# Regrouping the sorted rows of a mixture of experts, its lookahead and its indirect DMAs

## The chip, the cores and the metric

The kernel runs on one core of one Trainium2 chip, in float32. The metric is the device time of one execution in microseconds. Engines: PE (TensorE, matmuls and transposes), DVE (VectorE), ACT (ScalarE), POOL (GpSimd), and SP, which issues DMAs. PEld is PE's loading of weights beside its matmuls. DMAs issued by SP and ACT have descriptors made by hardware; the indirect ones (a row for each of 128 indices) are issued by POOL, in software.

## The reference, cut to what matters

Four layers work on X, 8 sequences of 256 tokens with 128 features, 16 heads of 8. Each normalises X first and adds its result to it.

```python
x = x + attn_a(layernorm(x))     # layer 0: attention with rotated q, k, v
x = x + ffn(layernorm(x))        # layer 1
x = x + attn_b(layernorm(x))     # layer 2: attention on covariances
x = x + ffn(layernorm(x))        # layer 3, the same weights as layer 1

def ffn(x):
    h = x + attention(layer_norm(x))          # a plain attention of its own
    return h + moe(layer_norm(h))
def moe(t):                                   # t: 2048 tokens
    probs = softmax(t @ w_gate)               # 8 experts
    tw, ti = top_k(probs, 2); tw /= tw.sum()
    out = sum over e of weight(e) * (gelu(t @ w1[e] + b1[e]) @ w2[e] + b2[e])   # 128 -> 512 -> 128
```

Only the two chosen experts of a token have a weight that is not zero.

## The kernel before, in words

There are two **passes** (`ph` 0 and 1) of the same build: an attention part over 16 sequences (8 of an attention layer, then 8 of the ffn's attention: layers 0 and 1, then 2 and 3), and a **mixture** part. Every engine's program is written out by hand in its own order, and semaphores (`need`, `wait_ge`, `then_inc`) join them; an engine executes its instructions in order, so a wait holds all that is queued behind it.

**Attention.** `sequences(ph, s)` gives for step s six sequences u, t, a, m, n, p at six stages of a pipeline: p is normalised (statistics on DVE, the rest on POOL in `norm`, written as Zhl), n is transposed (`do_zT`), projected (`do_proj`) and its K, Q, V stacked by POOL and turned (`do_kT`, `do_qT`), m has raw scores made on PE (`do_raw`) and their maxima taken on DVE (`do_max`), a has scores (`do_scores`), exponentials on ACT and products with V (`do_pv`), t is divided, turned (`do_onT`) and projected (`do_wo`), and u is normalised for the mixture (`close` on POOL, `do_uT` on PE). For an ffn layer u also gets its gate: `do_gate` makes the logits; for each **block** of two sequences DVE's `choose` finds the two best, ACT's `do_gate_exp` takes an exponential, and `weigh` makes weights (WE, SH) and one-hot choices (OH). `timely(u)` leaves the last three sequences' gates to the mixture. A step is 8 slots of PE work. The maxima are turned (`do_mT`, L466), copied by ACT and written into rows of QT by a small DMA of SP (`set_shift`); the scores wait for it. PE, ACT and DVE run steps 0 to 18 in the first pass and 3 to 18 in the second (the first three are in the mixture's `fill`); POOL runs all 21 steps. Step 17 has a and m, and no n; step 18 has a, and neither m nor n.

**Sorting.** The choices of one **half** (4 sequences, 16 groups of 128 rows) are sorted by expert. PE's `do_rank` makes totals (part 0) and ranks (part 1), DVE turns them into a slot for each row (SLOT, in `first_rows` and `sort_rows`) and an expert for each tile of 128 sorted rows (EID, in `name_tiles`): 23 tiles a half (`NTL`), 46 in all (`NAT`), some of them filled up. POOL's `scatter(ph, half)` then writes U to `sorted_u` in memory, by 16 indirect DMAs (L1594). For the first half this is done in step 17 (`ranks`) with the scatter after POOL's step 17, for the second half in the mixture's `drain` (tiles 8 to 10).

**Mixture.** For each tile `at`: SP reads its rows (`load_x`, L373, 64 KB, 6 buffers XT) and its expert's first weights (`load_w`, L383, 258 KB, 5 buffers W1; it reads the expert's number from EID and waits for the activations of the tile whose buffer it takes). PE turns the rows (`turn_x`, L688), ACT copies them with scale and bias (`copy_x`, XTT, 2 buffers), PE makes the first products (`hidden`, L697, 8 matmul records), ACT the four Gelus (G, 2 buffers), PE the second products (`outputs`, L710, 8 records), DVE copies them out (`evacuate`, Yb, 3 buffers), and ACT issues the write to `sorted_y` (`store`, L962). PSUM: `ring_e` is four banks that ACT frees, `ring_r` three banks that DVE frees. PE's order is: turn tile at+2, first products of at+1, second products of at. Between the tiles lie `drain` (the rest of this pass: gates, the second half's ranks, b2) and, in the first pass's second half, `fill` (the front of the next attention layer, for sequences 0 and 1).

**Gathers.** POOL's `gather(ph, b)` reads the two expert rows of each token of sequence b back by 4 indirect DMAs (L1610) into 8 buffers Yg; the first of a half waits until all its stores have landed. DVE's `combine` weighs and adds them to X; in layer 2 the norm of sequence b needs it. Gathers of sequences 0 and 1 come before POOL's first step of the second pass, 2 to 7 in its steps: behind the stacks of n, ahead of the norm of p (b = p+1), so four of them in attention steps of the second pass proper.

## Time and profile before

| | us |
|---|---|
| runs: median of 3 (lowest, highest) | 967.03 (964.18, 973.73) |
| the profiled execution | 970.91 |
| its span (first to last instruction) | 969.1 |
| PE busy | 803.9 (83%) |
| ACT busy | 576.6 (60%) |
| DVE busy | 545.4 (56%) |
| POOL busy | 481.1 (50%) |
| mean granted clock of PE | 0.871 of full speed |

The rows below come from one profiled execution, 3.9 us above the median of the runs, with 1.8 us around its span. Times are us from the span's start. A row of the timeline has: start, duration, engine, line, operation, output<-input, shapes, the number of instructions merged in it, and in square brackets how long the engine stood idle before it and what ended that; "remote" is a releaser that the profile doesn't know, "issue" means that it waited for nothing that is shown. A granted clock of 1.00 is 2.4 GHz and 0.50 is 1.2 GHz. The first pass's attention goes to about 328.7, its mixture to 482.5, the second pass's attention to 798.2, its mixture to 941.4, and the last gathers and the output to the end.

### The profile page before, as it was taken

The numbers are of one execution on the slowest core, as the hardware profiler recorded it, in microseconds if no ns is written. First come the engines' busy times: TensorE is split into PE (matmuls) and PEld (weight loads), VectorE is DVE, ScalarE is ACT, GpSimd is POOL, SyncE is SP. The second block draws the span as 40 slices with busy tenths as digits, with TensorE's granted clock in tenths as the row PEclk, the third lists the DMA queues.
The fourth block names the chain that finished last, engine by engine and source line by source line (L and its number), as shares of the span: only waits on it lengthen the run. The fifth ranks groups of instructions, "written<-read, shape, count | busy, mean of one in ns | idle before, by whom it ended". The sixth has DMA issues, their size and how long they took to land.

```text
span 969.1 us, 21562 instructions
## 1 busy us (share of the span) xinstructions
PE 803.9 (83%) x7166; PEld 574.7 (59%) x7166; DVE 545.4 (56%) x1370; ACT 576.6 (60%) x1336; POOL 481.1 (50%) x906
## 2 busy tenths in 40 slices
PE   2999999999985983879878989999998599666780
PEld 2755556666652783878745556666665258566680
DVE  4799988788872230023656768788887322210122
ACT  1377767878752681555555556787876248444460
POOL 6667777577635215045444456366763621412305
PEclk9999989999965896889978889999998558878895
DMA  9200000000001452555200000000000124435552
GB/s 288 68 3 2 3 2 3 3 3 3 3 13 34 121 155 84 134 147 147 59 13 13 14 13 2 3 2 3 3 3 5 42 75 126 132 101 154 145 135 65
DMA packets 58746, 56.31 MB, mean 58 GB/s; under 512 B 7944, under 2 KB 43536, under 8 KB 58640
## 3 DMA queue, kind: packets, MB, share of 16 engines
q1 hardware_dynamic: 40288, 39.13, 15.0%
q0 software_dynamic: 4096, 8.40, 3.0%
q10 hardware_dynamic: 14256, 7.41, 2.6%
q8 instruction: 61, 1.00, 0.4%
q14 instruction: 45, 0.37, 0.1%
HBM read 40.10 MB, written 14.29 MB: 56 GB/s over the span
## 4 chain that ended last, share of the span: by engine, by line
PE 56%; DVE 17%; POOL 8%; issue 7%; another core or an unknown queue 7%; ACT 4%; DMA 1%; ACTq 1%; POOLq 0%; DVEq 0%; SPq 0%
PE bankO L456 11%; DVE M L1112 9%; PE bankE L697 8%; PE bankR L710 8%; PE bankE L475 7%; PE bankE L429 6%; PE bankR L442 3%; POOL Yg L1610 3%; DVE QKV L1074 2%; PE bankE L466 2%; ACT G L951 2%; PE bankR L526 2%; PE bankR L544 2%; PE bankR L496 1%
## 5 line engine op out<-in xcount | busy, mean ns | idle before, releaser
L1112 DVE TENSOR_REDUCE M<-bankR 128x2 f32<-128x512 f32 x512 | 326.5, 684 | 113.1 <-PE bankR L442 76.9
L838 ACT ACTIVATE Pr<-bankE 128x512 f32<-128x512 f32 x512 | 276.9, 595 | 128.2 <-PE bankE L429 119.8
L442 PE MATMUL bankR<-KQ 32*128 32x256 f32 x1024 | 181.6, 349 | 17.5 <-DVE M L1112 13.7
L456 PE MATMUL bankO<-Pr,Vx 128*32 128x256 f32 x2048 | 179.7, 427 | 5.9 <-ACT OT L832 5.9
L429 PEld LDWEIGHTS bankE<-KQ 32*128 32x128 f32 x1024 | 85.3, 199 | 108.7 <-issue 72.4
L1327 DVE COPY Yb<-bankR 128x128 f32<-128x128 f32 x92 | 26.6, 290 | 208.7 <-PE bankR L710 137.5
L429 PE MATMUL bankE<-KQ 32*128 32x256 f32 x1024 | 141.6, 350 | 1.7 <-issue 0.6
L951 ACT ACTIVATE G<-bankE,W 128x128 f32<-128x128 f32 x368 | 105.0, 371 | 56.7 <-PE bankE L697 35.6
L442 PEld LDWEIGHTS bankR<-KQ 32*128 32x128 f32 x1024 | 117.2, 198 | 32.2 <-DVE M L1112 27.3
L710 PE MATMUL bankR<-w,G 128*128 x736 | 107.9, 294 | 27.0 <-ACT G L951 23.7
L1610 POOL DMA_INDIRECT Yg<-sorted_y,SLOT x64 | 61.8, 966 | 126.6 <-DMA sorted_y<-Yb 97.3
L697 PE MATMUL bankE<-XTT,W 128*128 128x128 f32 x736 | 110.0, 298 | 13.6 <-ACT XTT L943 7.2
L710 PEld LDWEIGHTS bankR<-w,G 128*128 128x128 f32 x736 | 98.3, 208 | 30.0 <-issue 30.0
L697 PEld LDWEIGHTS bankE<-XTT,W 128*128 128x128 f32 x736 | 101.8, 214 | 16.0 <-ACT XTT L943 8.8
L1594 POOL DMA_INDIRECT sorted_u<-U,SLOT x64 | 62.1, 971 | 87.5 <-DVE past L1307 56.6
L832 ACT ACTIVATE KQ<-bankE 128x512 fp32r<-128x512 f32 x128 | 71.2, 606 | 21.5 <-PE bankE L475 19.9
L943 ACT ACTIVATE XTT<-bankE,lncols 128x128 f32<-128x128 f32 x92 | 42.4, 463 | 45.3 <-PE bankE L688 31.4
L456 PEld LDWEIGHTS bankO<-Pr,Vx 128*32 128x32 f32 x2048 | 42.6, 113 | 43.4 <-issue 21.0
L1511 POOL CAST Kst<-QKV 128x512 fp32r<-128x512 f32 x24 | 15.7, 653 | 92.2 <-DVE QKV L1072 52.4
L1436 POOL TENSOR_SCALAR lnsmall<-meanvar 128x2 f32<-128x2 f32 x48 | 11.0, 230 | 93.7 <-DVE meanvar L1042 91.2
L475 PE MATMUL bankE<-ident_r,Kst 128*128 128x256 f32 (+1 forms) x256 | 40.6, 306 | 4.1 <-POOL Kst L1514 4.1
L475 PE MATMUL bankE<-ident_r,Zhl 128*128 128x256 f32 (+1 forms) x128 | 25.4, 329 | 20.7 <-POOL X L1482 12.9
(169 smaller groups left out, 1169.4 us busy)
## 6 DMA issues: line engine op xcount, KB each, us to landing
W<-in_w1b SPq DMA_DIRECT2D x92, 258.0 KB
XT<-sorted_u SPq DMA_DIRECT2D x92, 64.0 KB
sorted_y<-Yb ACTq DMA_DIRECT2D x92, 64.0 KB
sorted_u<-Yg SPq DMA_DIRECT2D x2, 1472.0 KB, 9.6
KQ<-MT SPq DMA_DIRECT2D x128, 4.0 KB
X<-in_x SPq DMA_DIRECT2D x8, 128.0 KB, 6.5
sorted_u<-U,SLOT POOLq DMA_INDIRECT x64
Yg<-sorted_y,SLOT POOLq DMA_INDIRECT x64
```

The source lines that it names most:

```text
L429: k = mm(act_bank("S", layer, b, h)[:, z * T:z * T + T], KT[rows, kb, g, z * P:z * P + P], QT[rows, kb, g, :], start=True, stop=True)
L442: k = mm(dve_bank("raw", layer, b, h)[:, z * T:z * T + T], QT[rows, kb, g, z * P:z * P + P], KT[rows, kb, g, :], start=True, stop=True)
L456: k = mm(bankO[SL * j:SL * j + SL, cols], Vx[:, b % VB, kc, HG * g + j, :], Pr[:, g % 2, j, kc, :], start=(g % 2 == 0 and kc == 0), stop=( ...
L475: return mm(bank[:, i * P:i * P + n], src, ident_r[:, 0:n], start=True, stop=True)
L697: k = mm(act_bank("hid", ph, at)[:, c * P:c * P + P], W1[:, n % NW, c * P:c * P + P], XTT[:, n % 2, :], start=True, stop=True)
L710: k = mm(dve_bank("out", ph, at)[:, 0:D], G[:, (ph * NAT + at) % 2, c, :], w2[:, bass.ds(e * FC + c, 1), :].rearrange("p o d -> p (o d)"), ...
L832: return nc.scalar.activation(dst, src, ACT.Copy)
L838: nc.scalar.activation(Pr[:, (h // HG) % 2, h % HG], act_bank("S", layer, b, h).rearrange("p (k q) -> p k q", k=TT), ACT.Exp, scale=EXP_SC ...
L951: nc.scalar.activation(G[:, n % 2, c, :], act_bank("hid", ph, at)[:, c * P:c * P + P], ACT.Gelu_apprx_tanh, bias=W1[:, n % NW, FF + c:FF + ...
L1112: v.tensor_reduce(M[:, b % 2, :, h], dve_bank("raw", layer, b, h).rearrange("p (t k) -> p t k", t=TT), AX.X, ALU.max, negate=True).then_in ...
L1594: g.indirect_dma_start(sorted_u[half][:, :], bass.IndirectOffsetOnAxis(ap=SLOT[:, half, n:n + 1], axis=0), U[:, b, t, :], None).then_inc(s ...
L1610: g.indirect_dma_start(Yg[:, n % NYG], None, sorted_y[half][:, :], bass.IndirectOffsetOnAxis(ap=SLOT[:, half, at:at + 1], axis=0)).then_in ...
```

## The change

It touches these places:

- **Groups of four.** Rows are read, turned and copied in groups (`GROUP`): six a half, of 4, 4, 4, 4, 4 and 3 tiles. One DMA brings up to 256 KB, PE turns a group into one bank of `ring_e` by four transposes, and ACT copies it in one instruction. XT and XTT have two groups each. `group_at(at)` is the group that is turned during tile at, six tiles before its first.
- **Lookahead.** PE makes first products three tiles ahead (`LEAD`), beginning anew in each half; ACT's Gelus run two tiles ahead in its order, into 5 buffers G; 7 buffers W1; `store` of a tile is issued four tiles later (`LAG`), with 6 buffers Yb.
- **SP's order.** Seven weight loads, four groups of rows (the third and fourth wait for `x_turned` of the first two), then weights seven tiles ahead; the second half's four groups are asked for at tile 18.
- **First half's ranks and writes.** Totals after step 17, ranks and slots in step 18 (in the slot of `do_mT(a, 1)` and behind the last maxima), and POOL's `scatter(ph, 0)` after its step 18.
- **Gates.** `timely` goes, so sequence 5's gate, and with it block 2's `choose` and `do_gate_exp`, are in step 18, and its `weigh` begins DVE's mixture. Within a step `do_uT` and `do_gate` come later, `weigh` always a step after `choose`, and `do_gate_exp` after the last exponentials.
- **Drain and fill** are spread otherwise over the tiles (ranks at 9 and 10, weT and b2 at 12 to 19; zT, projections, K, Q, raw scores and combines of `fill` moved by up to some tiles).
- **Gathers** come behind the norm in POOL's step.

```diff
-NX, NW, NY, NYG = 6, 5, 3, 8
+LEAD = 3
+LAG = 4
+NXG, NW, NGB, NY, NYG = 2, 7, 5, 6, 8
+XG = 4
+GROUP = [(half * NTL + i, min(XG, NTL - i)) for half in range(2) for i in range(0, NTL, XG)]
+NGRP = len(GROUP)
+GROUP_OF = {first: q for q, (first, _) in enumerate(GROUP)}
...
-        G = sb("G", [P, 2, FC, P])
+        G = sb("G", [P, NGB, FC, P])
...
-        XT = sb("XT", [P, NX, D])
-        XTT = sb("XTT", [P, 2, P])
+        XT = sb("XT", [P, NXG, XG, D])
+        XTT = sb("XTT", [P, 2, XG, P])
...
-        def timely(u):
-
-            return None if u and LAYERS[u[0]] == "ffn" and u[1] >= NB - 3 else u
+        def group_at(at):
+
+            return GROUP_OF.get(at + XG + 2) if at % NTL + XG + 2 < NTL else None
...
-            def load_x(ph, at):
-
-                half, i = divmod(at, NTL)
-                k = (ph * NAT + at) % NX
+            def load_x(ph, q):
+
+                half, i = divmod(GROUP[q][0], NTL)
+                n, k = GROUP[q][1], (ph * NGRP + q) % NXG
                 if i == 0:
                     sp.wait_ge(scattered[half], 16 * GROUPS * (ph + 1))
-                need(sp, x_turned, ph, at - NX)
-                sp.dma_start(XT[:, k], sorted_u[half][i * P:i * P + P, :]).then_inc(x_in[k], 16)
+                need(sp, x_turned, ph, q - NXG)
+                sp.dma_start(XT[:, k, 0:n, :],
+                             sorted_u[half][i * P:(i + n) * P, :].rearrange("(j p) d -> p j d", p=P)).then_inc(x_in[k], 16)
...
-                def begin(half):
-                    for i in range(NW - 1):
-                        load_w(ph, half * NTL + i)
-                    for i in range(NX - 1):
-                        load_x(ph, half * NTL + i)
-
-                for half in range(2):
-                    begin(half)
-                    for i in range(NTL):
-                        at = half * NTL + i
-                        if i + NX - 1 < NTL:
-                            load_x(ph, at + NX - 1)
-                        if i + NW - 1 < NTL:
-                            load_w(ph, at + NW - 1)
+                for at in range(NW):
+                    load_w(ph, at)
+                for q in range(2 * NXG):
+                    load_x(ph, q)
+                for at in range(NAT):
+                    if at + NW < NAT:
+                        load_w(ph, at + NW)
+                    if group_at(at - 1) is not None and group_at(at - 1) % (NGRP // 2) < NGRP // 2 - NXG:
+                        load_x(ph, group_at(at - 1) + NXG)
+                    if at == NTL - XG - 1:
+                        for q in range(NGRP // 2, NGRP // 2 + 2 * NXG):
+                            load_x(ph, q)
...
                     do_mT(*a, 1)
-                if ranks:
-                    do_rank(m[0] // 2, 0, 0)
+                if a and LAYERS[a[0]] == "ffn" and a[1] == NB - 1:
+                    do_rank(a[0] // 2, 0, 1)
...
+            def turn_x(ph, q):
+                x = ph * NGRP + q
+                pe.wait_ge(x_in[x % NXG], 16 * (x // NXG + 1))
+                ring_e.take(pe, ("x", ph, q))
+                for j in range(GROUP[q][1]):
+                    k = turn(act_bank("x", ph, q)[:, j * P:j * P + P], XT[:, x % NXG, j, :], ident[:])
+                k.then_inc(x_turned.sem, 1)
+                ring_e.give(("x", ph, q), x_copied, ph, q)
 
             def hidden(ph, at):
                 n = ph * NAT + at
-                need(pe, x_copied, ph, at)
+                q, j = group_of(at)
+                if j == 0:
+                    need(pe, x_copied, ph, q)
...
                 if i == 1:
-                    do_uT(layer, NB - 3)
-                if i == 2:
-                    do_gate(layer, NB - 3)
                     do_uT(layer, NB - 2)
-                if i == 3:
+                if i == 4:
                     do_gate(layer, NB - 2)
-                if i == 4:
                     do_uT(layer, NB - 1)
-                if i == 5:
+                if i == 6:
                     do_gate(layer, NB - 1)
-                if i == 8:
+                if i == 9:
                     do_rank(ph, 1, 0)
-                if i == 9:
+                if i == 10:
                     do_rank(ph, 1, 1)
-                if i in (10, 12):
-                    do_weT(ph, i // 2 - 3)
-                if i in (11, 13):
-                    do_b2(ph, i // 2 - 3)
+                if i in (12, 16):
+                    do_weT(ph, i // 4 - 1)
+                if i in (15, 19):
+                    do_b2(ph, (i - 3) // 4 - 1)
...
-                turn_x(ph, 0)
-                turn_x(ph, 1)
-                hidden(ph, 0)
-                for at in range(NAT):
-                    if at + 2 < NAT:
-                        turn_x(ph, at + 2)
-                    if at + 1 < NAT:
-                        hidden(ph, at + 1)
-                    outputs(ph, at)
-                    drain(ph, at)
-                    if ph == 0:
-                        fill(layer + 1, at - NTL)
+                for half in range(2):
+                    turn_x(ph, half * NGRP // 2)
+                    turn_x(ph, half * NGRP // 2 + 1)
+                    for at in range(half * NTL, half * NTL + LEAD):
+                        hidden(ph, at)
+                    for at in range(half * NTL, half * NTL + NTL):
+                        if at % NTL + LEAD < NTL:
+                            hidden(ph, at + LEAD)
+                        outputs(ph, at)
+                        if group_at(at) is not None:
+                            turn_x(ph, group_at(at))
+                        drain(ph, at)
+                        if ph == 0:
+                            fill(layer + 1, at - NTL)
...
                     step(*sequences(ph, s))
+                    if s == STEPS - DRAIN - 2:
+                        do_rank(ph, 0, 0)
...
+            def copy_x(ph, q):
+
+                n = GROUP[q][1]
+                need(act, x_turned, ph, q)
+                if q >= 2:
+                    need(act, hid, ph, sum(GROUP[q - 2]) - 1)
+                elif ph:
+                    need(act, hid, ph - 1, sum(GROUP[q - 2 + NGRP]) - 1)
+                nc.scalar.activation(XTT[:, (ph * NGRP + q) % 2, 0:n, :].rearrange("p j r -> p (j r)"),
+                                     act_bank("x", ph, q)[:, 0:n * P], ACT.Identity, bias=lncols[:, 3:4],
+                                     scale=lncols[:, 2:3]).then_inc(x_copied.sem, 1)
...
+                for half in range(2):
+                    for x in range(2):
+                        copy_x(ph, half * NGRP // 2 + x)
+                        hidden(ph, half * NTL + x)
+                    for at in range(half * NTL, half * NTL + NTL):
+                        if at % NTL + 2 < NTL:
+                            hidden(ph, at + 2)
+                        if group_at(at) is not None:
+                            copy_x(ph, group_at(at))
+                        if at >= LAG:
+                            store(ph, at - LAG)
+                        drain(ph, at)
+                        if ph == 0:
+                            fill(layer + 1, at - NTL)
+                for at in range(NAT - LAG, NAT):
+                    store(ph, at)
...
                 if a:
                     do_max(*a, 7)
+                if a and LAYERS[a[0]] == "ffn" and a[1] == NB - 1:
+                    sort_rows(a[0] // 2, 0)
...
-                if block_of(gone) == (0, 0) or block_of(gone) == (1, 0):
+                if u:
+                    do_gate(*u)
+                if block_of(gone) is not None:
                     weigh(*block_of(gone))
+                if block_of(u) is not None:
+                    choose(*block_of(u))
                 if m:
                     do_max(*m, 6)
-                if block_of(u) == (0, 1) or block_of(u) == (1, 1):
-                    weigh(*block_of(u))
...
                 if n:
                     stack_q(*n)
                     stack_v(*n)
+                if p and not early:
+                    norm(*p)
                 if p and p[0] == 2 and 0 < p[1] < NB - 1:
                     gather(0, p[1] + 1)
-                if p and not early:
...
                     step(*sequences(ph, s))
-                    if s == STEPS - DRAIN - 2:
+                    if s == STEPS - DRAIN - 1:
                         scatter(ph, 0)
```

## Rows read from the trace of the kernel before

**Rows 1.** Windows by stage: busy PE, PEld, DVE, ACT, POOL; clock; DMA share, GB/s

```profile
257.00:273.60 16.60, 16.27 (x180) 10.28 (x176) 14.29 (x48) 13.16 (x29) 5.70 (x12) 1.00 0.01 3
273.60:309.10 35.50, 22.16 (x142) 12.17 (x142) 14.94 (x37) 9.76 (x21) 18.55 (x23) 0.51 0.09 31
309.10:328.70 19.60, 19.34 (x155) 10.05 (x155) 5.51 (x18) 11.57 (x24) 5.91 (x14) 0.75 0.32 89
...
535.50:558.00 22.50, 20.85 (x176) 12.59 (x171) 16.04 (x34) 13.46 (x28) 12.04 (x23) 0.85 0.05 14
579.50:597.80 18.30, 17.90 (x169) 11.12 (x168) 16.00 (x37) 12.86 (x27) 11.70 (x30) 0.91 0.01 2
```

**Rows 2.** Timeline of step 17 of the first pass, at its burst of writes

```profile
283.87 1.23 POOL L1594 DMA_INDIRECT sorted_u<-U,SLOT  x1 [6.75 <-DVE SLOT L1303]
...
291.03 0.69 PE L536 MATMUL bankE<-ident,On 128*128 128x128 f32 x2
...
299.90 0.69 DVE L1112 TENSOR_REDUCE M<-bankR 128x2 f32<-128x512 f32 x1 [9.30 <-remote]
...
303.08 0.96 POOL L1594 DMA_INDIRECT sorted_u<-U,SLOT  x1 [0.30 <-issue]
305.55 0.38 ACT L832 ACTIVATE OnT<-bankE 128x256 f32<-128x256 f32 x1 [7.21 <-remote]
```

**Rows 3.** Timeline of the first mixture, at the second burst of writes

```profile
364.80 0.60 PE L720 MATMUL bankE<-ident,WE 128*8 128x128 f32 x4
...
379.27 0.96 POOL L1594 DMA_INDIRECT sorted_u<-U,SLOT  x1 [0.30 <-issue]
...
383.08 0.59 ACT L832 ACTIVATE WT<-bankE 8x512 f32<-8x512 f32 x1 [11.55 <-remote]
```

**Rows 4.** Timeline of the first mixture, first products of two undisturbed tiles

```profile
391.91 1.06 PE L697 MATMUL bankE<-XTT,W 128*128 128x128 f32 x8
...
393.81 1.06 PE L697 MATMUL bankE<-XTT,W 128*128 128x128 f32 x8
```

**Rows 5.** Windows, second products (L710) alone, 8 to a tile: PE, PEld; clock; DMA

```profile
334.10:365.00 30.90, 12.87 (x96) 11.67 (x96) 1.00 0.62 170
365.00:389.60 24.60, 3.98 (x16) 3.60 (x16) 0.60 0.24 70
...
401.40:408.70 7.30, 1.93 (x9) 1.83 (x8) 0.69 0.49 138
...
419.30:431.80 12.50, 2.88 (x17) 2.69 (x16) 0.73 0.48 127
```

**Rows 6.** Timeline of steps 17 and 18: slots, maxima turned, first product

```profile
283.38 0.17 DVE L1303 CAST SLOT<-place 128x16 uint32<-128x16 f32 x1
...
310.93 0.59 PE L466 MATMUL bankE<-ident,M 128*8 128x128 f32 x2
...
329.52 2.07 PE L697 MATMUL bankE<-XTT,W 128*128 128x128 f32 x8 [0.44 <-ACT XTT L943]
```

**Rows 7.** Timeline where the halves meet: reads of rows and their turn

```profile
402.41 2.75 SPq L373 DMA_DIRECT2D XT<-sorted_u  x6
...
404.84 0.48 PE L688 MATMUL bankE<-ident,XT 128*128 128x128 f32 x1 [3.40 <-DMA XT<-sorted_u]
```

**Rows 8.** Timeline of the first mixture, a table load for the gate

```profile
340.96 1.28 ACT L930 ACT_TABLE_LOAD   x1
```

**Rows 9.** Timeline of one step with four gathers

```profile
534.85 0.61 POOL L1511 CAST Kst<-QKV 128x512 fp32r<-128x512 f32 x1 [7.13 <-DVE QKV L1072]
...
541.78 1.09 POOL L1610 DMA_INDIRECT Yg<-sorted_y,SLOT  x1 [0.15 <-issue]
...
543.72 0.30 DVE L1042 BATCH_NORM_AGGREGATE meanvar<-stats 128x2 f32<-128x6 f32 x2
...
546.72 0.24 POOL L1436 TENSOR_SCALAR lnsmall<-meanvar 128x2 f32<-128x2 f32 x1
...
550.78 1.05 PE L475 MATMUL bankE<-ident_r,Zhl 128*128 128x256 f32 x4 [0.93 <-POOL Zhl L1477]
```

More of the change, by code:

```diff
@@ L323, in block_of, with group_of @@
             return (u[0] // 2, u[1] // 2) if u and LAYERS[u[0]] == "ffn" and u[1] % 2 else None
-        def timely(u):
-            return None if u and LAYERS[u[0]] == "ffn" and u[1] >= NB - 3 else u
+        def group_at(at):
+            return GROUP_OF.get(at + XG + 2) if at % NTL + XG + 2 < NTL else None
+        def group_of(at):
+            q = max(q for q, (first, _) in enumerate(GROUP) if first <= at)
+            return q, at - GROUP[q][0]
         def own_steps(ph):
@@ L697, in hidden @@
                     k = mm(act_bank("hid", ph, at)[:, c * P:c * P + P], W1[:, n % NW, c * P:c * P + P],
-                           XTT[:, n % 2, :], start=True, stop=True)
+                           XTT[:, (ph * NGRP + q) % 2, j, :], start=True, stop=True)
                 k.then_inc(hid.sem, 1)
@@ L900, in step @@
                     do_exp(*a, 3)
+                    do_exp(*a, 4)
                 if u:
@@ L997, in mixture @@
                 do_weT(ph, 1)
                 do_onT(layer, NB - 1)
-                copy_x(ph, 0)
-                copy_x(ph, 1)
-                hidden(ph, 0)
-                for at in range(NAT):
-                    if at + 2 < NAT:
-                        copy_x(ph, at + 2)
-                    if at + 1 < NAT:
-                        hidden(ph, at + 1)
-                    if at:
-                        store(ph, at - 1)
-                    drain(ph, at)
-                    if ph == 0:
-                        fill(layer + 1, at - NTL)
@@ L1271, in copy_totals, with sort_rows, done @@
                 v.tensor_copy(totals[:], dve_bank("totals", ph, half)[:, 0:P]).then_inc(sorted_.sem, 1)
-            def first_rows(ph, half):
+            def sort_rows(ph, half):
                 bank = dve_bank("rank", ph, half)
+                def done(x):
+                    need(dve, sorted_, ph, half, x)
                 need(dve, ranked, ph, half)
@@ L1588, in scatter @@
                 if ph:
-                    need(pool, x_turned, ph - 1, NTL * half + NTL - 1)
+                    need(pool, x_turned, ph - 1, (half + 1) * NGRP // 2 - 1)
                 else:
```

207 lines of the change are left out of this document (65 added, 142 removed).

## The prediction

> **What bounds the kernel now.** I read the page first, then the stages as windows, then the order of time inside the longest stages. Over the whole span PE is busy for 83% and no other engine for over 60%, so the shares say little. The windows by stage say more [rows 1]. An ordinary attention step of the second pass takes 18.30 us when no rows are gathered in it (579.5 to 597.8). The last but one own step of the first pass takes 35.50 us (273.6 to 309.1) although PE is busy for 22 of them, at half clock (mean 0.51), and its twin of the second pass as long. POOL issues 16 indirect writes there, one each 1.26 us, from 283.87 to 304.04 [rows 2]. What the other engines do in that time is the key. PE has finished the onT turn at 291.7, and ACT copies it only at 305.55; DVE takes up the maxima of the same slot at 299.90, after an idle time of 9.30. Both waits are put down to no known releaser, and the last ends as the burst ends. Nothing that they wait for is a DMA.
>
> The burst for the second half shows the same [rows 3]: PE turns WE at 364.80, ACT copies it at 383.08, 3 us after POOL's last write was issued at 379.27. So this trace shows a **hold**: some 6 to 7 us after a burst of indirect DMAs begins, PE's signals reach DVE and ACT many microseconds late, and this ends with the burst. A burst of 16 costs nearly its whole length; one of 4 ends before the hold begins.
>
> Inside the mixture an undisturbed tile takes 1.90 us (first products of two tiles at 391.91 and 393.81 [rows 4]), and PE has no gap in it: its matmuls are the bound. The windows that count second products (8 to a tile) show where tiles take longer [rows 5]: 12 tiles in 30.90 us while the drain goes on (8.1 more than 12 x 1.90); 2 tiles in 24.60 under the second scatter (20.8 more); 1 tile in 7.30 where the halves meet (5.4 more); 2 tiles in 12.50 under the first 8 gathers (8.7 more). The second pass has the same pattern, within 1 us in each place.
>
> **The change part by part**, all against the profiled execution's 970.91 us.
>
> *First half's writes.* The rank chain leaves step 17 and the 16 writes follow step 18. Step 17 has then no burst: its POOL has only one close. It has no new block (no zT, projection, kT, qT), so it has less to do than the 16.60 us step before it [rows 1]; against that stands the clock, which was at half over this step. I take 17 us for it, between 13 (less work at full clock) and 21 (half clock: 10.3 us went before the burst, for half of the step [rows 1, 2]). Gain 18.6 us a pass, 37 in all.
>
> Step 18 pays. Its maxima are reduced and turned 1.8 us after its start (309.1 to 310.93 [rows 6]); the rank products and the ten small DVE operations behind them take about 4.7 us (some 0.3 each with its gap; the last is the 0.17 us cast [rows 6]), so the burst begins 6.5 us into the step and ends after 20.2 more, at 26.7. Today the step and what follows it last 19.6 us until the first rows are turned [rows 1], and the first product starts at 329.52 [rows 6]. The last shift DMA goes out before the slots are known, so attention itself waits for no transfer. With a hold as in step 17, some 6 us of the remaining 13 get done before it, and 6.8 after its end: 33.5 us. The rows can be read only when the last write has landed: 26.7 + 1.5, and then two groups of four tiles; a 64 KB read started at 402.41 was turned at 404.84 [rows 7]; eight tiles are 512 KB, at 138 to 170 GB/s [rows 5] 3 to 4 us: 31.7 us. So the two ends are close together, the hold sets it, and step 18 with what stands behind it grows from 19.6 to 33.5: a loss of 14 us a pass, 28 in all. What is hidden: seven weight loads (1.8 MB, 11 us at 170 GB/s [rows 5]) run under the burst. If they don't run under it, the groups of rows queue behind them on SP, 8 us later. Net of both: 9 us gained, between -10 and +22.
>
> *Drain.* Block 2's gate goes into step 18, so one pair of table loads (2 x 1.28 us on ACT [rows 8]) and one uT and gate leave the loop. The other pair meets a PE that runs three tiles ahead. ACT's four row copies become one, so it catches up. Of the 8.1 us, 4 go and 4 stay (PE's own products): 8 us for both passes, between 4 and 12.
>
> *Lookahead under the hold.* Five G buffers and three tiles ahead let PE do two more tiles before it runs dry, 2 x 1.90 us. The three bankR banks stay, and a held DVE doesn't empty them; so I take 3 us of the 20.8, a pass: 6, between 0 and 10. LAG of 4 with 6 Yb buffers lets ACT no longer stand at a store.
>
> *Where the halves meet.* Today the six reads go out at 402.41 only, behind weight loads that wait for activations, and PE waits 3.40 us [rows 7]. Now groups 6 and 7 are asked for at tile 18. But SP then stands at group 8 (x_turned of group 6) with the loads of tile 26 on behind it, and tile 26 is asked for three tiles earlier than before: perhaps 2 us of wait. I take 2.4 of 5.4 us, a pass. *First gathers.* The store of tile 22 goes out later by two tiles in PE's order, the gathers with it, and DVE stands at its combine. In the first pass the chain store, gather, combine, norm, zT binds soon behind, so 1 us of the 8.7 goes; in the second no zT follows and lookahead covers more: 4.6. Sum 10 us (2.4 + 1, 2.4 + 4.6), between 0 and 18.
>
> *Gathers behind the norm.* In four steps of the second pass POOL issues four gathers (541.78 to 546.6) before a norm whose statistics are there at 544.0; it starts at 546.72, and PE then waits for Zhl (0.93 us before 550.78, and the clock is at 0.85 over the step) [rows 1, 9]. These steps take 22.50 against 18.30 us [rows 1]. Moved, the norm starts 2.6 us sooner and the gathers fall into POOL's idle time before the next K stack (7.13 us before 534.85 [rows 9]), which covers 5.05 us. Part of the 4.2 us is the combine, which stays: 2 us a step, 8 in all, between 2 and 14. If that cover were short, the K stack would be late by the rest. The other moves (uT, gate, weigh and gate_exp by a slot or two, fill by some tiles) carry the same instructions into idle time of the same engines: 0, within 5 us each way.
>
> Sum: 37 - 28 + 8 + 6 + 10 + 8 = 41, so 970.91 - 41 = 930. The median of the runs is 967.03, 3.9 below the profiled one: **926**.
>
> **The rivals.** (a) *The hold bites less in step 18.* Less remains to be signalled there, so the start is set by the landed rows, 31.7 or sooner, and step 17 takes 14.5; that is 2 x 1.8 and 2 x 2.5 more, and the lookahead's terms come out 10 higher: 907. For it: the attention steps already fit 4 gathers without any hold. Against it: both bursts of 16 held alike. (b) *Lookahead gives little*, because DVE is held and three bankR banks stop PE as before, and SP stands at group 8: the terms of 6, 10 and 8 shrink to 3 together, 947. (c) *The scatter wasn't what held step 17.* Then step 17 stays at 33 us (half clock, a slow chain), and the first products now wait for the scatter, behind seven weight loads: start at 31.7 + 8 us of step 18 against 19.6, a loss of 20 a pass, 40 in all; 5 from step 17, 8 + 3 + 8 elsewhere. That is 16 slower: 983. It decides as soon as step 18 and its tail take over 20 us more than now while step 17 stays above 30. Against it stand the waits that end with the bursts, twice in each pass.
>
> The Trainium skill (DMA: Bandwidth & Descriptors, section SWDGE vs HWDGE vs iDMA) says that software- and hardware-generated descriptors sit in different queues of each DMA engine, served in turn, and that HWDGE transfers are immune to what disturbs the software rings. By that rule alone a burst would cost the others nothing but its share of the queues, and (c) would be the outcome. The trace disagrees for signals between engines: PE, DVE and ACT wait without any DMA in between [rows 2, 3].
>
> **How the numbers follow.** My forecast 0.58, (a) 0.17, (b) 0.14, (c) 0.07, no visible effect because gains and losses cancel 0.04. The bounds of the terms give the forecast some 20 us each way; (a) and (b) lie within or near that. Range 898 to 956. A change of under 1% (10 us) can't be told from none with this kernel. Faster by over 1% means below 957.4: the forecast, (a), and nearly all of (b), 0.86; within 1% 0.07; slower 0.07.
>
> **What would show it.** Step 17 of each pass at 13 to 21 us without long waits for an unknown releaser; POOL's 16 writes inside the last step, waits of 5 us and more on ACT or DVE there, and the first product 31 to 35 us after that step's start. In the mixture 12 drain tiles in some 27 us, the pair under the second scatter still near 21 us, the meeting of the halves near 5. The four gather steps near 20 us with gathers after Zhl. The forecast is wrong if step 17 stays above 25, if the first product waits for XT or W long after the last write, or if SP's wait at group 8 leaves PE waiting for weights for more than a few us.

## The result and the profile after

| | before | after |
|---|---|---|
| runs: median (lowest, highest) | 966.04 (964.18, 973.73), 4 runs | 921.47 (916.59, 923.03), 4 runs |
| ratio, 95% interval | | 0.9516 (0.9451 to 0.958) |
| the profiled execution, its span | 970.91, 969.1 | 916.59, 914.8 |
| PE busy | 803.9 (83%) | 769.5 (84%) |
| mean granted clock of PE | 0.871 | 0.912 |

The change makes the kernel 4.8% faster, at 4.5 us from the forecast median of 926. The profiled execution of before is 4.9 us above its median and that of after 4.9 below, so the traces differ by 54.3 us of span where the medians differ by 44.6. The forecast's 41 was worked out on the traces: set against 54.3 it is 13 short, and only against the medians 3.6 short. That the median was met within 4.5 us is in part luck. A ratio leaves disturbed runs out, so it can differ from the quotient of the medians; for the kernel before on the third chip of the experiments that leaves out 10 of 24 runs, and the median of the others is 870.5 us.

The windows of after, by step (17, 18, tail up to about the last residual sum of attention) and by tiles, each counted from the end of one tile's second products to the end of another's (12 of the drain, 8 under the second burst, 4 where the halves meet); the columns are those of [rows 1]:

```profile
270.00:283.30 13.30, 12.54 (x150) 6.62 (x150) 12.70 (x34) 10.40 (x22) 2.97 (x7) 1.00 0.02 4
283.30:312.90 29.60, 14.24 (x134) 7.61 (x132) 7.73 (x39) 10.78 (x22) 18.55 (x23) 0.73 0.35 101
312.90:320.40 7.50, 7.50 (x48) 4.89 (x45) 4.20 (x18) 1.94 (x4) 2.98 (x7) 0.70 0.21 64
327.30:353.40 26.10, 25.19 (x226) 24.98 (x226) 8.65 (x48) 18.28 (x55) 1.01 (x1) 1.00 0.61 173
353.40:386.60 33.20, 23.63 (x149) 20.75 (x148) 3.56 (x10) 10.34 (x35) 14.45 (x16) 0.74 0.38 107
386.60:397.40 10.80, 9.42 (x80) 8.81 (x79) 1.17 (x5) 6.61 (x22) 0.00 (x0) 1.00 0.62 173
```

Step 17 has shrunk from 35.5 us to 13.3 and has its full clock; step 18, to which the burst has moved, takes 29.6 with PE busy for 14 of them. Its timeline:

```profile
290.10 1.23 POOL L1557 DMA_INDIRECT sorted_u<-U,SLOT  x1 [2.24 <-DVE past L1289]
...
308.64 0.60 ACT L834 ACTIVATE Pr<-bankE 128x512 f32<-128x512 f32 x1 [9.52 <-remote]
309.32 0.96 POOL L1557 DMA_INDIRECT sorted_u<-U,SLOT  x1 [0.30 <-issue]
311.45 0.60 ACT L834 ACTIVATE Pr<-bankE 128x512 f32<-128x512 f32 x1 [2.21 <-remote]
311.57 10.18 SPq L384 DMA_DIRECT2D XT<-sorted_u  x4
312.89 0.42 DVE L1127 TENSOR_TENSOR Hs<-bankR,Hs 128x256 f32<-128x256 f32 x1 [15.77 <-remote]
...
320.21 1.04 PE L695 MATMUL bankE<-ident,XT 128*128 128x128 f32 x8
```

These answer to [rows 2]: the same waits for an unknown releaser, in another step. The second burst answers to [rows 3]. Read PE's rows here as well:

```profile
359.52 0.27 PE L707 MATMUL bankE<-XTT,W 128*128 128x128 f32 x1 [1.05 <-issue]
360.93 0.27 PE L707 MATMUL bankE<-XTT,W 128*128 128x128 f32 x1 [1.14 <-issue]
...
363.11 0.29 DVE L1309 COPY Yb<-bankR 128x128 f32<-128x128 f32 x1 [9.40 <-remote]
...
371.47 0.96 POOL L1557 DMA_INDIRECT sorted_u<-U,SLOT  x1 [0.31 <-issue]
...
373.68 1.10 PE L707 MATMUL bankE<-XTT,W 128*128 128x128 f32 x3 [1.03 <-issue]
375.13 0.53 DVE L1309 COPY Yb<-bankR 128x128 f32<-128x128 f32 x2 [11.73 <-remote]
375.18 0.67 ACT L942 ACTIVATE XTT<-bankE,lncols 128x384 f32<-128x384 f32 x1 [16.58 <-remote]
```

Single matmuls start 0.7 or 1.4 us apart with "issue" ahead of them. So the hold is not only late signals, as the prediction had it: PE's own issue is slow as well, from 5 to 6 us after the first write to 3 to 4 us after the last. Whether the "remote" waits of DVE and ACT are late signals, or these engines too take up their instructions late, the traces don't tell apart.

### The profile page after: what moved, and what is told of

Its sections match the earlier page's. It is cut to its first block, busy times and chain, and to the rows that moved or that the text cites. A ratio compares the mean times of both kernels' runs of the same rounds, so it can differ in the third digit from the quotient of the medians.

```text
span 914.8 us, 21285 instructions
## 1 busy us (share of the span) xinstructions
PE 769.5 (84%) x7166; PEld 549.2 (60%) x7166; DVE 544.5 (60%) x1370; ACT 543.8 (59%) x1264; POOL 481.0 (53%) x906
## 4 chain that ended last, share of the span: by engine, by line
PE 57%; DVE 19%; issue 9%; POOL 6%; another core or an unknown queue 3%; DMA 2%; ACT 2%; SPq 0%; ACTq 0%; POOLq 0%; DVEq 0%
PE bankO L466 11%; DVE M L1106 11%; PE bankR L720 8%; PE bankE L485 8%; PE bankE L707 7%; PE bankE L439 6%; PE bankR L452 3%; POOL Yg L1573 3%; DVE QKV L1068 2%; PE bankE L476 2%; PE bankR L536 2%; PE bankR L506 1%; PE bankR L554 1%; PE bankR L738 1%
## 5 line engine op out<-in xcount | busy, mean ns | idle before, releaser
L466 PE MATMUL bankO<-Pr,Vx 128*32 128x256 f32 x2048 | 170.5, 406 | 18.0 <-issue 11.0
L452 PE MATMUL bankR<-KQ 32*128 32x256 f32 x1024 | 172.4, 340 | 10.1 <-DVE QKV L1066 4.4
L439 PEld LDWEIGHTS bankE<-KQ 32*128 32x128 f32 x1024 | 79.6, 188 | 96.3 <-issue 63.7
L439 PE MATMUL bankE<-KQ 32*128 32x256 f32 x1024 | 132.8, 335 | 0.0
L707 PE MATMUL bankE<-XTT,W 128*128 128x128 f32 x736 | 105.5, 286 | 23.0 <-issue 14.0
L452 PEld LDWEIGHTS bankR<-KQ 32*128 32x128 f32 x1024 | 110.9, 191 | 22.8 <-DVE M L1106 11.9
L951 ACT ACTIVATE G<-bankE,W 128x128 f32<-128x128 f32 x368 | 101.2, 387 | 26.6 <-PE bankE L707 16.4
L707 PEld LDWEIGHTS bankE<-XTT,W 128*128 128x128 f32 x736 | 94.7, 199 | 27.0 <-issue 21.1
L720 PEld LDWEIGHTS bankR<-w,G 128*128 128x128 f32 x736 | 95.9, 203 | 15.2 <-issue 14.8
L466 PEld LDWEIGHTS bankO<-Pr,Vx 128*32 128x32 f32 x2048 | 41.1, 110 | 54.5 <-issue 29.6
L942 ACT ACTIVATE XTT<-bankE,lncols 128x512 f32<-128x512 f32 (+1 forms) x24 | 18.3, 763 | 75.5 <-remote 38.5
L485 PE MATMUL bankE<-ident_r,Zhl 128*128 128x256 f32 (+1 forms) x128 | 23.8, 312 | 24.0 <-POOL X L1445 13.5
```

Of the source, the lines that this page charges most:

```text
L439: k = mm(act_bank("S", layer, b, h)[:, z * T:z * T + T], KT[rows, kb, g, z * P:z * P + P], QT[rows, kb, g, :], start=True, stop=True)
L452: k = mm(dve_bank("raw", layer, b, h)[:, z * T:z * T + T], QT[rows, kb, g, z * P:z * P + P], KT[rows, kb, g, :], start=True, stop=True)
L466: k = mm(bankO[SL * j:SL * j + SL, cols], Vx[:, b % VB, kc, HG * g + j, :], Pr[:, g % 2, j, kc, :], start=(g % 2 == 0 and kc == 0), stop=( ...
L485: return mm(bank[:, i * P:i * P + n], src, ident_r[:, 0:n], start=True, stop=True)
L707: k = mm(act_bank("hid", ph, at)[:, c * P:c * P + P], W1[:, n % NW, c * P:c * P + P], XTT[:, (ph * NGRP + q) % 2, j, :], start=True, stop= ...
L720: k = mm(dve_bank("out", ph, at)[:, 0:D], G[:, (ph * NAT + at) % NGB, c, :], w2[:, bass.ds(e * FC + c, 1), :].rearrange("p o d -> p (o d)" ...
```

## The experiments

Three groups of four ran, each group on a chip of its own beside the kernel before, which took 967.42, 963.78 and 873.77 us there; part 4 is about the third figure. "More" and "less" without a name is against the 921.47 of after, which was not run again beside them; for the first two groups the kernel before (966.04 beside after) says that this shifts a difference by 1 to 2 us.

**1. Terms of the change, one at a time.**

*Gathers ahead of the norm again*, in POOL's step:

```diff
-                if p and not early:
-                    norm(*p)
                 if p and p[0] == 2 and 0 < p[1] < NB - 1:
                     gather(0, p[1] + 1)
+                if p and not early:
+                    norm(*p)
```

> The changed kernel with the gathers ahead of the norm in POOL's step, as in the kernel before. Theory: the gather steps of the second pass are late by the norm's delay, 8 to 11 us in all, so about 930. Rival (the shorter steps there come from the new fill order, not from the gathers' place): within 3 us of 921.

931.57 us (927.25 to 935.84), ratio 0.9637 (0.9575 to 0.9698): 10 more than after. In its trace three of the steps take 22.9, 23.6 and 19.9 us, against 19.3, 21.3 and 20.3: theory met.

*One tile of lookahead*:

```diff
-LEAD = 3
+LEAD = 1
```

> The changed kernel with first products only one tile ahead on PE (LEAD 1); buffers stay. Theory: PE runs dry two tiles earlier in each hold and meets the table loads of the gate uncovered: the 17 us stall under the second burst goes back to 19 to 21, the drain gets 2 to 3 us longer, in each pass; 8 to 16 us slower than the changed kernel, about 932. Rival (lookahead gives nothing, the gains there are the lighter drain and the groups): within 3 us of 921.

934.97 us (930.78 to 937.78), ratio 0.9667 (0.9606 to 0.9728): 13.5 more, theory met in size. In the trace of each pass the 12 tiles of the drain take 29.3 us for 26.1, the 8 under the second burst 34.4 and 34.6 for 33.2, and the second half's tiles 4 us more; the stretch between the halves gets 2 us shorter. So lookahead is worth little under the hold itself.

*First half's ranks and writes in step 17 again* (core of the edit; the sort, its totals and one `weigh` move with it):

```diff
+                if ranks:
+                    do_rank(m[0] // 2, 0, 0)
...
-                    if s == STEPS - DRAIN - 1:
+                    if s == STEPS - DRAIN - 2:
                         scatter(ph, 0)
```

> The changed kernel with the first half's ranks and writes back in step 17, all else as changed. Theory: the hold of the burst is then in step 17 again (35 us for 13.3) and out of step 18 and the tail (21 for 37), and the first tile comes out 4 to 6 us later in each pass: 930 to 934 us. Rival: the place of the burst is worth nothing and the other edits made the gain: 921 us. A second rival: the writes land earlier and the rows are there when attention ends, which is worth more than the hold costs: 915 us.

944.49 us (939.26 to 946.99), ratio 0.977 (0.9703 to 0.9838). Direction right, but 23 more than after where 9 to 13 were expected. The burst holds step 17 as before (35.2 and 36.0 us), and steps 18 take 18.0. Before took 14.4 and 16.5, but had no gate of sequence 5 in step 18; here DVE stands 5.9 us for its logits (`LG` of PE). How much of the step that accounts for was not separated. The three edits undone one at a time cost 10, 13.5 and 23 us, 46.6 in all, and the whole change gives 44.6: if they add, little is left for the parts that no run took back.

**2. The hold and the length of a run of writes.** In `scatter`, POOL waits after each four writes until they have landed; first for the second half alone, then for both:

```diff
                 for n in range(GROUPS):
+                    if half and n and n % 4 == 0:        # both halves: without "half and"
+                        pool.wait_ge(scattered[half], 16 * (GROUPS * ph + n))
```

> The changed kernel, with one more wait: POOL issues the second half's 16 writes in fours and waits for each four to land before the next. Theory (a hold begins some 6 to 7 us after a burst begins and lasts to its end; a burst of four is over before it begins): the 17 us that two tiles lose under this burst in each pass shrink to 2 or 3, the rows land 8 us later, which no one waits for, and the time falls by 28 us to about 893. Rival (every indirect DMA takes its 1 us from the others, wherever it lies): no gain, 921, within 5 us. Second rival (the hold comes from the count of writes in flight or done, not from the length of an unbroken burst): the stall is spread over the four groups and the time stays within 10 us of 921.

909.12 us (908.41 to 910.28), ratio 0.9394 (0.9338 to 0.945): 12 better than after, between theory (893) and rival (921). The trace of this kernel shows why:

```profile
352.90:370.80 17.90, 17.65 (x148) 16.55 (x145) 2.93 (x9) 9.92 (x35) 10.02 (x12) 1.00 0.52 148
```
```profile
358.88 0.96 POOL L1559 DMA_INDIRECT sorted_u<-U,SLOT  x1 [2.02 <-DMA sorted_u<-U,SLOT]
...
366.74 0.95 POOL L1559 DMA_INDIRECT sorted_u<-U,SLOT  x1 [3.12 <-DMA sorted_u<-U,SLOT]
...
379.04 5.49 SPq L384 DMA_DIRECT2D XT<-sorted_u  x4
...
383.16 0.78 ACT L942 ACTIVATE XTT<-bankE,lncols 128x512 f32<-128x512 f32 x1 [13.80 <-PE bankE L695]
```

The eight tiles that took 33.2 us take 17.9 (18.2 in the second pass), with PE idle for 0.3: the hold is gone but for a rest of under 1 us (part 4), some 15 us a pass. But the second half's rows are read at 379.04, as they were in after (379.21, where SP stood behind the weights of held tiles), and the tile loop, now early, waits for them: 15.8 us between the last tile of one half and the first of the other, where after had 7.2. The hold had covered this wait, which the theory had put at nothing ("no one waits for" the rows).

> The changed kernel with both halves' writes in fours, each four waiting until the four before have landed. With the second half alone paced it took 909. Theory: step 18 falls from 29.6 us to 15 to 18, since short runs of writes hold nothing; but the last write lands later (each wait costs some 2 to 3 us, so 6 to 7 in all), and the first product waits for rows in place of the hold: the first tile comes out as before within 4 us, 905 to 917 us in all, 912 likeliest. Rival: attention's end sets the first tile, and the 12 us of hold are won in each pass: 889 us.

908.90 us (906.47 to 909.36), ratio 0.9409 (0.9352 to 0.9467), the theory's time. Step 18 takes 14.8 us instead of 29.6:

```profile
283.20:298.00 14.80, 13.01 (x122) 7.34 (x124) 7.75 (x39) 10.55 (x22) 7.19 (x12) 0.89 0.35 97
```
```profile
316.48 5.27 SPq L384 DMA_DIRECT2D XT<-sorted_u  x4
...
319.40 1.97 PE L695 MATMUL bankE<-ident,XT 128*128 128x128 f32 x8 [10.62 <-DMA XT<-sorted_u]
```

and PE then waits 10.62 us for the rows: first tile at 328.0, after 327.3. The rows are also later here: they are asked for at 316.48, in after at 311.57, since the pacing holds back the last write by 4.9 us. In after the first rows had landed at 314.4 (2.8 us from issue to landing), 5.8 us before PE came to turn them at 320.21. So in after the hold sets the first tile, with the rows ready 5 to 6 us earlier, and the pacing spends what it saves. How it is with neither hold nor pacing, a kernel of part 4 shows (the one in runs of eight, whose first half is not paced):

```profile
313.84 1.97 PE L695 MATMUL bankE<-ident,XT 128*128 128x128 f32 x8 [11.64 <-DMA XT<-sorted_u]
```

Its first tile comes 52.8 us after the start of step 17, that of after 57.3: 4.5 us of hold that could be had there.

Step 18 isn't free of the hold either with runs of four. It took 14.8 and 16.1 us here, and 12.3 in both passes of the kernel of part 4 that also has both halves in fours. The longest wait of this trace for an unknown releaser there has PE as its releaser in the other, and 2.3 us:

```profile
DVE LG L1133 <- remote: 4.5, 1, 4.5
```

*Only 8 of the second half's 16 writes* (rows of the others are left as they were, so part of the computation is missing):

```diff
-                for n in range(GROUPS):
+                for n in range(GROUPS if half == 0 else GROUPS // 2):
```

> The changed kernel with only 8 of the 16 writes of the second half (the other rows of that half keep what stood there: part of the computation is left out). Theory: the hold comes of a long unbroken run of writes, so that the first four cost next to nothing and what is held is from about 6 us after the first write to the last one. 8 writes take 10 us, so 3 to 4 us of the hold of 15 stay in each pass; the second half's rows are there in time too, and the wait for them at the meeting goes: 893 us. Rival: each write costs its share (15 us by 16 writes), 7.5 us of it stay, 900 us. In the trace the 8 tiles from the 12th take 21 us by the first and 25 by the second, against 33.2.

907.74 us (906.17 to 912.50), ratio 0.942 (0.9359 to 0.9482). The theory misses: the 8 tiles take 25.8 us, 7.9 over the 17.9 of the paced run, which is half of 15.3, as the rival had it (25, though not its 900 us in all). That each write costs its share wherever it stands is still not so, since 16 writes in fours cost these tiles next to nothing. Ten us of writes (351.68 to 361.6) hold from about 357.5 to 366: a hold begins 5 to 6 us late and ends 4 late, and a run of four is over before it has begun in earnest.

*Gathers in runs, too* (on top of the first pacing; each of the sequences 1 to 3 waits for the gathers of the one before):

```diff
+                if b in (1, 2, 3):
+                    for n in range((ph * NB + b - 1) * 2 * TT, (ph * NB + b) * 2 * TT):
+                        pool.wait_ge(y_in[n % NYG], 16 * (n // NYG + 1))
```

> The kernel with the paced writes of the second half, and POOL also waits for the landing of one sequence's four gathers before it issues the next sequence's, for sequences 1 to 3 of each pass. Theory: the 12 us that tiles lose under the first eight gathers in each pass shrink to some 4, partly eaten in the first pass by the chain gather, combine, norm, zT, which gets 2 us longer; about 12 us below the run with paced writes alone, so about 881. Rival (a fixed toll per indirect DMA): no gain over the run with paced writes alone, or 2 to 4 us slower.

913.19 us (907.38 to 914.57), ratio 0.942 (0.9353 to 0.9487): no gain, a miss, as the rival had it. In the second pass the stall of 12.3 us in one tile is replaced by 7.6, 5.9 and smaller ones, since each sequence's combine, and DVE's copies of tiles behind it, now stand behind later gathers.

**3. Writes in fours, and in step 17** (the edit above with the one of part 1):

> Both halves' writes in fours as in the run beside it, and the first half's ranks and writes in step 17. Theory: with the hold gone, an earlier burst costs nothing and its rows land before attention has ended, so that both the hold and the wait for rows go: step 17 15 us, step 18 15, tail 7, the first tile some 8 us earlier in each pass than with the second half paced alone: 894 us. Rival: short runs in step 17 still hold attention (its steps need a signal between engines every 0.3 us or so, where the tiles need one in 2), step 17 is 22 us or more: 905 us or above.

917.20 us (913.40 to 920.39), ratio 0.9501 (0.9437 to 0.9566). The theory (894) fails: 20.6 and 26.2 us for steps 17 and 18, near the rival's 22 and 905 or above. The waits of this kernel in them:

```profile
DVE LG L1134 <- PE bankR L573: 12.5, 1, 12.5
POOL lnsmall L1403 <- DVE meanvar L1037: 9.2, 1, 9.2
...
PEld bankE L564 <- POOL U L1414: 6.8, 1, 6.8
POOL sorted_u L1563 <- DVE past L1295: 6.5, 1, 6.5
```

These are known releasers. PE's weight load waits 6.8 us for U of sequence 5, which POOL normalises behind its burst, and the paced burst ends at 307.5. A queue took the place of the hold. The 20.6 us of step 17 are no hold either, in the main: the kernel before in fours (part 4) has 20.0 and 21.3 there on a chip that holds nothing.

**4. Another chip.** The third group was to test the slots of uT and gate, the pacing in the kernel before, an earlier second burst, and two runs of eight.

```diff
                 if m:
                     do_raw(*m, 3)
-                if u:
-                    do_uT(*u)
                 if a:
                     do_pv(*a, 1, 0)
```

(and uT, the gate, its exponential and `choose` in their old slots)

> The changed kernel with uT, the gate, its exponential and the choice back in the slots of an attention step that they had before; weigh stays where the change put it. Theory: the two steps of each pass that carry them go back from 16.1 to about 17.1 us, 4.9 us in all: 926 us. Rival: the steps got shorter because the first half's ranks left them or because of weigh, and the slots are worth nothing: 921 us.

868.34 us (864.80 to 871.29), ratio 0.998 (0.995 to 1.001).

> The kernel before with both halves' writes in fours, each four waiting for the landing of the four before; nothing of the change in it. Theory: in the drain the hold of the second burst goes (12 us a pass fewer) and half of it comes back as a wait for rows; in step 17 the burst in fours keeps GpSimd for 24 us, and what the step needs from GpSimd stands behind it, as in the changed kernel with its writes there (20.6 and 26.3 us for steps 17 and 18 against 35.8 and 14.4), which gains 3 a pass: 948 us. Rival: the hold was all that the change avoided, and the old kernel with the pacing is as fast as the new one: 921 us or less.

890.86 us (890.41 to 895.31), ratio 1.0261 (1.019 to 1.0332).

```diff
-                if i == 9:
+                if i == 7:
                     do_rank(ph, 1, 0)
```

(and likewise the other steps named)

> The changed kernel with both halves in fours, and the last two gates, the weights and the second half's ranks one to two tiles earlier in the drain (gates at 3 and 5 for 4 and 6, weigh at 6 for 8, ranks at 7 and 8 for 9 and 10). Theory: with the hold gone, the tile loop waits 10 to 12 us a pass for the second half's rows; the burst begins two tiles (4 to 5 us) sooner and the wait is so much shorter: 909 less 9, 900 us. Rival: the rows' wait is set by something else (the weights' loads, or the short runs now collide with the copies of the first tiles): 909 us.

878.94 us (874.49 to 883.12), ratio 1.0111 (1.0054 to 1.0168).

```diff
+                    if half and n == 8:
+                        pool.wait_ge(scattered[half], 16 * (GROUPS * ph + n))
```

> The changed kernel with the second half's writes in two runs of eight, the second waiting for the landing of the first. With runs of four it took 909; one run of eight alone held the tiles for 7.9 us, and sixteen in a row for 15.3. Theory: a run holds the others from about 5 us after its first write to 4 us after its last one, so that fours hold next to nothing and two eights hold as much as sixteen in a row: 921 us, and a stall in each run. Rival: what counts is that the queue is let run dry once in a while, and one pause takes most of the hold away: 912 us.

867.70 us (866.44 to 871.17), ratio 0.9982 (0.9951 to 1.0013).

No expected total can be judged, since all were reckoned from 921 and 909, and no theory on a hold can be tested, that of the runs of eight above all. The kernel before itself takes 873.77 here (864.58 to 889.90, 24 runs), some 90 less than on the two other chips. Its own runs lie 25 us apart, which nothing here explains, and those of the kernels beside it 5 to 9. The trace of the kernel with the old slots shows what is missing (step 17, step 18, eight tiles under the second burst, and three of that burst's rows):

```profile
272.60:286.80 14.20, 12.92 (x150) 6.99 (x150) 12.72 (x35) 10.87 (x22) 2.96 (x7) 1.00 0.01 3
286.80:299.20 12.40, 11.56 (x121) 6.76 (x124) 7.68 (x39) 10.10 (x22) 7.35 (x12) 1.00 0.23 62
352.70:369.90 17.20, 17.20 (x150) 16.59 (x148) 3.72 (x10) 10.17 (x35) 12.93 (x15) 1.00 0.60 167
```
```profile
353.17 0.96 POOL L1557 DMA_INDIRECT sorted_u<-U,SLOT  x1 [0.30 <-issue]
...
367.65 0.96 PEld L738 LDWEIGHTS bankR<-b,WT 8*128 8x128 f32 x8
...
370.84 0.96 POOL L1557 DMA_INDIRECT sorted_u<-U,SLOT  x1 [0.30 <-issue]
```

The burst is the same, 16 unbroken writes at one each 1.26 us; PE is busy for all of the 17.20 us, where after took 33.2. Step 18 takes 12.4 with its burst in it. **On this chip there is no hold.** The attention steps without indirect DMAs are the same on all three (15.5 us). Each chip was visited once, so whether it is the chip or something else about that visit, the runs don't say; "chip" below stands for both. The section of the Trainium skill that the prediction set against the trace (DMA: Bandwidth & Descriptors, SWDGE vs HWDGE vs iDMA) puts software and hardware descriptors in different queues of each DMA engine. By that alone, as the prediction worked out, a burst costs other engines nothing but its share of the queues: this trace agrees, and the traces of the two other chips show a cost to PE, ACT and DVE that this doesn't tell of.

What can be read here in steps and tiles: the old slots put back 17.1 us for 16.2 in one step and 14.2 for 13.2 in another, residual to residual; sequence 4's residual comes at 272.6 against 269.5 in the kernel with runs of eight. The first expectation holds in one of its two steps: the other stays at 16.2, and step 17 is longer in its place. The pacing gives nothing where nothing is held, and costs what the landing waits cost: the kernel with both halves paced and earlier ranks has its first tile at 327.2, that with runs of eight at 322.3. The earlier ranks did bring the second burst forward: first write at 347.2, rows read at 374.1, against 353.1 and 379.5 in the kernel with both halves paced of part 2. But the stretch between the halves stayed at 14.4 and 15.9 us (14.8 and 14.2 with runs of eight), so the wait for rows did not shrink as the theory had it; the tile loop came early by as much.

## Why the prediction was right, point by point

Terms for both passes, us of span:

| step of the prediction | forecast | measured |
|---|---|---|
| step 17 | -37 | -43.8 |
| step 18 and tail | +28 | +30.2 |
| drain, 12 tiles | -8 | -10.4 |
| lookahead under the second burst | -6 | -5.9 |
| halves meet, and first gathers | -10 | -10.5 |
| gathers behind the norm | -8 | -11.5 |
| other moves | 0 | -4.9 |
| start of the mixture, in none of the terms | 0 | +2.7 |
| sum with small rests | -41 | -54.3 |

The sum moved further than forecast by 13.3 us of span, mainly in step 17 (6.8), in moves put at 0 (4.9) and in the gather steps (3.5). The median hides this, since the profiled run of before lay above its median and that of after below.

- *First half's writes.* The mechanism was right: step 17 falls with its clock at 1.00, and the hold moves into step 18. Within the bound of 13 to 21 I took the middle; 13.3 is the end with the full clock. Rival (c) is dead: moved writes freed step 17, and writes put back held it again. Rival (a) was nearer in step 17 (14.5) and had the start of the mixture wrong.
- *Step 18.* Counted from the step's start (283.3), the burst begins after 6.8 us (forecast 6.5), SP can ask for the rows after 28.3 (forecast 28.2), the first rows have landed after 31.1 (forecast 31.7 for two groups), and PE turns them after 36.9 (forecast 33.5). So the hold sets it, as forecast, but it ends 3.4 us later, and the two ends are not as close together as the 1.8 us of the prediction. That the term came out at 30.2 for 28 all the same is in part luck: the forecast took 19.6 us for before in both passes, and in the second one before took some 24 up to its first turned rows. The burst slows SP as well: its seven weight loads go out over 12.7 us here, over 6.9 in the kernel with runs of eight on the chip without a hold, in time for the rows in both.
- *Drain, meeting, lookahead.* Within 2.5 us each. Rival (b), by which these shrink to 3 together, is out. The tile of 14.0 us under the first eight gathers stays in the first pass; it is no hold. PE waits 9.50 us there for the norm that POOL makes behind the gathers, and on the chip without a hold nearly as long:

```profile
404.27 1.12 PE L485 MATMUL bankE<-ident_r,Zhl 128*128 128x256 f32 x4 [8.75 <-POOL Zhl L1440]
```

  (kernel with runs of eight). In the second pass the next tile takes 12.6 us in after and 1.8 on that chip, so that one is the hold's.
- *Lookahead.* The term of 6 was for the hold alone, and its number is right (5.9), its reason only in part: with PE one tile ahead instead of three, the tiles under the hold get 1.2 and 1.4 us longer, 2.6 of the 5.9. What gives the rest (more G and W1 buffers, ACT's order, the groups) no run separates. The lead is worth 13.5 in all, most of it in the drain, a term of its own in the prediction, and in the second half's tiles, which no term had.
- *Gathers behind the norm.* Undone, +10; forecast 8.
- *Other moves.* The term forecast at 0 is worth 4.9, at its bound of 5. Some 3 of it are the new slots of uT and gate (the four steps up to sequence 4's residual take 65.8 us in each pass with the old slots, 64.4 without), and some 2 the first half's ranks, which are no "other move": with them back in step 17 the step before it takes 17.1 us for 16.0.
- *What failed:* the picture of the hold, in two points that the sum didn't use. PE's issue is held as well; and the hold was taken as a property of bursts, while it is one of bursts on some chips. Most of the change's gain seems to be avoided hold: on the third chip two kernels that differ little from the changed one are level with the kernel before. The changed kernel itself was not run there, nor is there a trace of the unpaced kernel before. What the parts are worth there can only be estimated, from the kernel before with writes in fours against the one with runs of eight. The first tile comes 46.5 us after step 17's start against 52.8, in the second pass 51.6 against 53.5, so the later burst costs some 6 and 2 us where nothing is held. The 12 tiles of the drain take 32.5 against 26.1, and 30.9 against 26.1, so the drain gives that back. Three gather steps take 24.6, 23.2 and 21.1 against 17.6, 17.5 and 18.0, so the gathers' place looks worth more there, not less. Where a gain of this size would be lost again, so that the totals come out level, stays open.

## What to carry to other kernels

Before a burst of indirect DMAs is moved or paced, ask what waits for its landing as well as what it disturbs: here the first tile was held 5.8 us longer than its rows took, and pacing, which removed the hold, delayed the rows by 4.9 and so gained nothing at that place. Where long runs of indirect DMAs hold other engines (idle times for an unknown releaser that end with the run), break them into fours that wait for their landing: a wait in the loop took some 15 us of stall out of each pass and gave 12 of the kernel's 921 us, but on a chip without the hold two kernels with both halves in fours were 1.1 and 2.6% slower than the kernel before. Run both kernels on several chips before such a change is called a gain: the same kernel took 967 and 874 us.

## What was unexpected of the hardware

- The hold depends on the chip: on two chips a run of 16 indirect writes of 128 rows holds PE, ACT and DVE for some 15 us, on the third for none, at the same rate of one write each 1.26 us. Its cause stays open: what differs between the chips, no trace here shows.
- It grows with the run: under 1 us over four runs of 4 writes in the tile loop (17.9 and 18.2 us on a chip with the hold, 17.2 on the one without), 7.9 us for 8, 15.3 for 16, beginning 5 to 6 us after the first write and ending 3 to 4 after the last. In attention's step 18 runs of four cost more: 14.8 and 16.1 us against 12.3.
- The steps with four gathers differ between the chips as well: 19.3 to 21.3 us at a clock of 0.83 to 0.92 in after, 17.5 to 18.0 at 1.00 in the kernel with runs of eight on the third chip. Over the four steps of after, these waits have no known releaser; over three such steps on the third chip there is no such wait at all:

```profile
DVE QKV L1066 <- remote: 4.1, 3, 2.0
ACT Pr L834 <- remote: 3.4, 2, 2.0
ACT OT L828 <- remote: 2.9, 2, 1.8
```

  So short runs hold other engines a little too, up to 2 us at a time. How much of the 2 to 3 us a step this makes was not measured.
